# Two stacked layers with sign masks and low-rank adapters: the adapter's A beside W1's columns, layer 2 in three parts of 1040 columns

## The chip, the cores and the metric

The kernel runs on one core of a Trainium2 chip. The metric is the device time of one execution in microseconds (us); three executions of the kernel before gave 435.9, 437.23 and 437.77 us, median 437.23 us.

## The reference

`x` is [8, 256, 1024] in float32. For each of the eight batches b:

```
x = x + x @ W0.T + b0 + coeff[b] * (x @ (2*mask[b, :1024, :1024] - 1))          # layer 1
h = x @ A[id[b]].T                                                             # [256, 16]
x = x + x @ W1.T + b1 + h @ B[id[b]].T                                         # layer 2
```

`A` and `B` are the rank-16 adapters of the batch's id, W0 and W1 are 1024 x 1024. Everything is float32 in and out. The mask has a full 1024 x 1024 table of integers for each batch.

## The kernel before

Every float32 operand of a large product is split into a high part that the fp32r format holds and a rest (`whi`/`wlo`, `xhl`, `yhl`, `w1hi`/`w1lo`); a product is then three products: high by high, high by low, low by high. Layer 1 runs transposed: a step n = 8b + c makes 128 of batch b's 1024 features, for all 256 rows. `layer1(n)` (L620) issues, for each of eight k, one product of 512 columns (L631: `whi` against x's high and low halves side by side) and one of 256 (L633: `wlo` against the high half). Layer 2 of a step (m = n - 1, one step behind) is `adapter_h(m)` (L638, one product of 512 columns, L641: A's columns against y's halves) and four `layer2(m, st, oh)` (L646), where st is one of two row tiles and oh one of two halves of the 1024 output columns: three products of 512 columns each (L657, L658, L659), accumulated over the eight steps of a batch in banks 0 to 3 of PSUM. So a step has 16 + 1 + 12 products.

Where m is the last step of a batch, `finish` (L663) adds B's part and the bias by one product of 512 columns for each bank (L669): its stationary operand `ht` holds h in parts (rows 0 to 31, 32 to 63, 64 to 79 and 96 to 111) and rows of ones for the bias, its moving operand `bt` B's rows. It waits for `ht`, which ScalarE (`h_parts_hi`, L386, three instructions) and VectorE (`h_parts_lo`, L518) cut out of bank HB (6) when `adapter_h` is done.

Around these products a step n has these instructions on the other two engines, in this order (c = n mod 8):

- VectorE: `make_w(n+2)` (L499, coeff*sign + W0 over 1024 columns), at c = 5 and 7 `rows_lo` (L482) for the next batch's x, `chunk_lo(n+2)` (L505, the rest of W), `make_y(n)` (L511), `y_parts_lo(n)` (L515, which raises `y_lo`), and at c = 4 and 6 `turn_rows` (L476, transposes half of the next batch's x).
- ScalarE: at c = 5 and 7 `rows_hi` (L362), `chunk_hi(n+2)` (L351), `half_y(n)` (L377, after `layer1(n)` is done), `sign(n+3)` (L344, after the mask has landed), `y_parts_hi(n)` (L384). At c = 0 the h parts come before `y_parts_hi`, and two `move_z` (L401) and the sign come after it; VectorE has its own two `move_z` (L527) there. `move_z` copies a finished bank of 512 columns to SBUF.

All queues are written out by hand and are in order. SP issues a mask per step (L171; `load_mask(n+4)` waits for `chunk_lo(n)`), at c = 0 four stores of 512 columns (L216), then the six transfers of the next `bt` (L206, L207), and at c = 2 the next batch's x. The order that TensorE's queue has for a step is

```
layer1(n, ...)                      # 16 products
adapter_h(m)                        # waits y_lo of step m = n - 1
layer2(m, 0, 0); layer2(m, 0, 1); layer2(m, 1, 0)
if m % KT == KT - 1: finish(m // KT, 0, 0); finish(m // KT, 0, 1); finish(m // KT, 1, 0)
layer2(m, 1, 1)
```

Of the kernel before, what the change touches and what calls it, by code (L numbers as in the profile page):

```python
# [11 lines left out]
P = 128  # L12
# [4 lines left out]
def two_layer_kernel(nc, x, coeff, ids, mask, W0, b0, W1, b1, lora_a, lora_b, out):  # L17
# [38 lines left out]

    with ExitStack() as ctx:
# [7 lines left out]
        w1hi = sb("w1hi", [P, KT, D], F32R)  # L65
        w1lo = sb("w1lo", [P, KT, D], F32R)
# [16 lines left out]
        zst = sb("zst", [P, 4, HALF])  # L83
# [4 lines left out]
        at = sb("at", [P, KT, (NB + 3) * 2 * R], F32R)  # L88
# [25 lines left out]
        z_stored = [sem(f"z_stored{j}") for j in range(4)]  # L114
# [25 lines left out]
        l2_done = sem("l2_done")  # L140
        h_done = sem("h_done")
        h_hi = sem("h_hi")
# [7 lines left out]
        def part_views(u, part):  # L150

            kind, c, h, bank = units[u]
            src = ps[:, bank, :]
            if kind == "w1":
                return (w1hi, w1lo)[part][:, c, h * HALF:(h + 1) * HALF], src
            if kind == "a":
                dst = at[:, 4 * h:4 * h + 4, 0:2 * P].rearrange("p k (b two r) -> p k b two r", b=NB, two=2)
                return dst[:, :, :, part, :], src.rearrange("p (k b r) -> p k b r", k=4, b=NB)
            dst = bhl[:, part, :].rearrange("p (m o) -> p o m", o=KT)[:, 4 * h:4 * h + 4, :]
            return dst, src.rearrange("p (o m) -> p o m", o=4)  # L160

        @block.sync
        def _(sp):
# [35 lines left out]
            def load_bt(b):  # L199
                if b == 0:  # L200
                    sp.wait_ge(parts_lo, parted(number["b", 0, 1]))
                else:
                    sp.wait_ge(z_done, 4 * b)
# [5 lines left out]
            def store_z(b, st, oh):  # L209
                if oh == 0:  # L210
                    sp.wait_ge(z_moved_act, 2 * b + st + 1)
                else:
                    sp.wait_ge(z_moved_dve, 2 * b + st + 1)
                j = 2 * st + oh
                dst = out[b, st * P:(st + 1) * P, oh * HALF:(oh + 1) * HALF]
                sp.dma_start(dst, zst[:, j, :]).then_inc(z_stored[j], 16)  # L216
# [16 lines left out]
            for n in range(NS):  # L233
# [9 lines left out]
                if c == 0 and b > 0:  # L243
                    for st in range(ST):
                        for oh in range(2):
                            store_z(b - 1, st, oh)
                    load_bt(b)
                if c == 2 and b + 1 < NB:
                    load_x(b + 1)
            for st in range(ST):  # L250
                for oh in range(2):
                    store_z(NB - 1, st, oh)
            for j in range(4):
                sp.wait_ge(z_stored[j], 16 * NB)

        @block.gpsimd
        def _(pool):
# [30 lines left out]

            nc.gpsimd.memset(ident[:, :], 0.0).then_inc(ident_set, 1)
# [5 lines left out]
            nc.gpsimd.memset(at[:, :, 2 * P:].bitcast(F32), 0.0).then_inc(consts_set, 1)  # L295
# [26 lines left out]
            eye_w1(7)  # L322

        @block.scalar
        def _(act):
# [60 lines left out]
            def h_parts_hi(b):  # L386
                act.wait_ge(h_done, b + 1)
                if b == 0:
                    act.wait_ge(consts_set, 3)
                else:  # L390
                    act.wait_ge(z_done, 4 * b)
                nc.scalar.activation(ht[0:2 * R, :], ps[0:2 * R, HB, 0:S], ACT.Copy).then_inc(h_hi, 1)
                nc.scalar.activation(ht[64:64 + R, :], ps[0:R, HB, S:2 * S], ACT.Copy).then_inc(h_hi, 1)
                act.wait_ge(h_hi, 3 * b + 1)
                nc.scalar.activation(ht[96:96 + R, :], ht[0:R, :].bitcast(F32), ACT.Copy).then_inc(h_hi, 1)

            def move_z(b, st):
                act.wait_ge(z_done, 4 * b + 2 * st + 1)
                if b > 0:
                    act.wait_ge(z_stored[2 * st], 16 * b)  # L400
                nc.scalar.activation(zst[:, 2 * st, :], ps[:, Z0 + 2 * st, :], ACT.Copy).then_inc(z_moved_act, 1)  # L401
# [42 lines left out]
            for n in range(KT, NS):  # L444
# [6 lines left out]
                if c == 0:  # L451
# [3 lines left out]
                y_parts_hi(n)  # L455
                if c == 0:
# [4 lines left out]
            move_z(NB - 1, 0)  # L461
            move_z(NB - 1, 1)

        @block.vector
        def _(dve):
# [52 lines left out]
            def h_parts_lo(b):  # L518
                dve.wait_ge(h_hi, 3 * b + 2)
# [3 lines left out]
            def move_z(b, st):  # L523
                dve.wait_ge(z_done, 4 * b + 2 * st + 2)
                if b > 0:
                    dve.wait_ge(z_stored[2 * st + 1], 16 * b)
                nc.vector.tensor_copy(zst[:, 2 * st + 1, :], ps[:, Z0 + 2 * st + 1, :]).then_inc(z_moved_dve, 1)  # L527
# [36 lines left out]
            for n in range(KT, NS):  # L564
# [8 lines left out]
                if c == 0:  # L573
                    h_parts_lo(b - 1)
                y_parts_lo(n)
                if c == 0:
                    move_z(b - 1, 0)
                    move_z(b - 1, 1)
# [3 lines left out]
            move_z(NB - 1, 0)  # L582
            move_z(NB - 1, 1)

        @block.tensor
        def _(pe):
# [59 lines left out]
            def layer2(n, st, oh):  # L646
                b, c = divmod(n, KT)
                j = 2 * st + oh
                if c == 0 and b > 0:
                    if oh == 0:  # L650
                        pe.wait_ge(z_moved_act, 2 * (b - 1) + st + 1)
                    else:
                        pe.wait_ge(z_moved_dve, 2 * (b - 1) + st + 1)
                hi = yhl[:, n % 2, st * P:(st + 1) * P]
                lo = yhl[:, n % 2, S + st * P:S + (st + 1) * P]
                cols = slice(oh * HALF, (oh + 1) * HALF)
# [6 lines left out]
            def finish(b, st, oh):  # L663
                if st == 0 and oh == 0:
                    pe.wait_ge(h_hi, 3 * (b + 1))
                    pe.wait_ge(h_lo, b + 1)
                    pe.wait_ge(bt_in, 96 * (b + 1))
                    pe.wait_ge(bias_moved, 32)
                nc.tensor.matmul(ps[:, Z0 + 2 * st + oh, :], ht[:, st * P:(st + 1) * P],  # L669
                                 bt[:, oh * HALF:(oh + 1) * HALF], start=False, stop=True).then_inc(z_done, 1)  # L670

# [9 lines left out]
            for n in range(NS + 1):  # L681
# [26 lines left out]
                if m == 0:  # L708
                    pe.wait_ge(consts_set, 3)
# [46 lines left out]
```

## Time and profile before

| | |
|---|---|
| three runs, median | 437.23 us |
| the profiled execution's own time | 436.89 us |
| its span, first to last instruction | 435.2 us |
| mean granted TensorE clock | 0.991 |
| PE busy | 407.3 us (94%) |
| VectorE busy | 283.1 us (65%) |
| ScalarE busy | 237.4 us (55%) |

PE is TensorE's matmul, PEld its weight load, DVE is VectorE, ACT ScalarE, SPq SyncE's queue of DMA issues. A product's start is exact in the trace, its end is modelled and overlaps the next product's; so the cost of a product is read from one start to the next. Layer 1 of step n ends where the step's next product starts.

### The profile page before, as it was taken

What the parts mean: (1) busy time and instruction counts of PE and PEld (TensorE: products, weight loads), DVE (VectorE), ACT (ScalarE), POOL (GpSimd) and SP (SyncE); (2) the same over time, 40 slices, a digit from 0 to 9 for tenths busy, and PEclk for the clock granted to TensorE, in tenths of its full rate; (3) what the DMA queues carried; (4) which work ended last, traced back from release to release, by engine and by line L of the source; (5) the groups of instructions that cost most, each with busy time, mean ns of one, the idle gap of its engine ahead of it and who ended that gap; (6) DMA issues with size and microseconds to landing.
All of it is one profiled execution on the core that took longest, in us unless ns stands there. A gap on an engine that the chain in (4) does not pass through costs nothing.

```text
span 435.2 us, 5517 instructions
## 1 busy us (share of the span) xinstructions
PE 407.3 (94%) x2049; PEld 341.0 (78%) x2049; DVE 283.1 (65%) x334; ACT 237.4 (55%) x352; POOL 25.2 (6%) x47
## 2 busy tenths in 40 slices
PE   3649999788999999999999999999999999999996
PEld 3538878566888888888888888888888888888885
DVE  0455757786578756886578657876588658865512
ACT  3366666636555645665455754565565555665412
POOL 4334410000000000000000000000000000000000
PEclk9997999999999999999999999999999999999999
DMA  7995694615973299218942496319911793246002
GB/s 232 244 331 157 211 229 134 146 48 128 217 175 98 76 201 234 69 39 203 228 125 62 122 234 165 98 48 224 243 52 50 185 251 104 77 116 163 2 0 97
DMA packets 90846, 63.29 MB, mean 145 GB/s; under 512 B 3515, under 2 KB 84419, under 8 KB 90820
## 3 DMA queue, kind: packets, MB, share of 16 engines
q1 hardware_dynamic: 89588, 59.28, 55.5%
q0 software_dynamic: 1232, 3.67, 2.5%
q8 instruction: 16, 0.26, 0.2%
q14 instruction: 10, 0.08, 0.1%
HBM read 51.39 MB, written 8.39 MB: 137 GB/s over the span
## 4 chain that ended last, share of the span: by engine, by line
PE 82%; DMA 5%; DVE 5%; SPq 4%; ACT 2%; issue 1%; ACTq 0%; DVEq 0%
PE ps L631 25%; PE ps L633 13%; PE ps L658 13%; PE ps L657 12%; PE ps L659 12%; DMA wm<-in_mask_Bx4096x_ik_dram 5%; PE ps L641 3%; PE ps L617 2%; PE ps L669 2%; SPq L183 1%; DVE wm L499 1%; DVE w1lo L471 1%; SPq L190 1%; DVE wlo L505 1%; SPq L226 1%
## 5 line engine op out<-in xcount | busy, mean ns | idle before, releaser
L631 PE MATMUL ps<-xhl,whi 128*128 128x512 f32 x512 | 187.6, 405 | 1.9 <-DVE wlo L505 1.1
L633 PE MATMUL ps<-xhl,wlo 128*128 128x256 f32 x512 | 144.9, 283 | 0.0
L631 PEld LDWEIGHTS ps<-xhl,whi 128*128 128x128 f32 x512 | 97.8, 191 | 24.9 <-DVE wlo L505 1.3
L505 DVE TENSOR_TENSOR wlo<-wm,whi 128x1024 fp32r<-128x1024 f32 x64 | 79.2, 1238 | 48.6 <-ACT whi L351 48.6
L351 ACT ACTIVATE whi<-wm 128x1024 fp32r<-128x1024 f32 x64 | 67.8, 1059 | 75.0 <-DVE wm L499 73.7
L657 PE MATMUL ps<-w1hi,yhl 128*128 128x512 f32 x256 | 101.5, 396 | 0.0
L658 PE MATMUL ps<-w1lo,yhl 128*128 128x512 f32 x256 | 100.6, 393 | 0.0
L659 PE MATMUL ps<-w1hi,yhl 128*128 128x512 f32 x256 | 100.4, 392 | 0.0
L633 PEld LDWEIGHTS ps<-xhl,wlo 128*128 128x128 f32 x512 | 98.1, 192 | 2.4
L499 DVE SCALAR_TENSOR_TENSOR wm<-wm,cs,w0t 128x1024 f32<-128x1024 f32 x64 | 81.6, 1275 | 23.4 <-ACT w0t L329 12.4
L344 ACT ACTIVATE wm<-wm 128x1024 f32<-128x1024 int32 x64 | 67.4, 1054 | 9.6 <-DMA wm<-in_mask_Bx4096x_ik_dram 9.5
L659 PEld LDWEIGHTS ps<-w1hi,yhl 128*128 128x128 f32 x256 | 48.1, 188 | 10.6
L658 PEld LDWEIGHTS ps<-w1lo,yhl 128*128 128x128 f32 x256 | 48.1, 188 | 10.5
L657 PEld LDWEIGHTS ps<-w1hi,yhl 128*128 128x128 f32 x256 | 48.2, 188 | 7.8
L515 DVE TENSOR_TENSOR yhl<-ysum,yhl 128x256 fp32r<-128x256 f32 x64 | 27.3, 427 | 36.6 <-ACT yhl L384 36.5
L377 ACT ACTIVATE ysum<-ps,b0col 128x256 f32<-128x256 f32 x64 | 30.0, 468 | 33.6 <-PE ps L633 33.2
L511 DVE TENSOR_TENSOR ysum<-ps,ysum 128x256 f32<-128x256 f32 x64 | 26.9, 420 | 13.8 <-ACT ysum L377 13.7
L362 ACT ACTIVATE xhl<-xt 128x1024 fp32r<-128x1024 f32 x14 | 14.9, 1061 | 31.1 <-DVE xt L476 31.1
L384 ACT ACTIVATE yhl<-ysum 128x256 fp32r<-128x256 f32 x64 | 26.4, 413 | 8.4 <-DVE ysum L511 8.2
L476 DVE STREAM_TRANSPOSE xt<-xraw 128x1024 f32<-128x1024 f32 x14 | 30.6, 2183 | 0.0
L641 PE MATMUL ps<-yhl,at 128*128 128x512 f32 x64 | 25.4, 397 | 0.0
L617 PE MATMUL ps<-ident,w0raw 128*128 128x128 f32 x64 | 11.6, 320 | 10.8 <-POOL w0raw L262 5.4
(49 smaller groups left out, 186.9 us busy)
## 6 DMA issues: line engine op xcount, KB each, us to landing
wm<-in_mask_Bx4096x_ik_dram SPq DMA_DIRECT2D x64, 512.0 KB, 5.7
out_dram<-zst SPq DMA_DIRECT2D x32, 256.0 KB, 2.5
xraw<-in_x_dram SPq DMA_DIRECT2D x28, 256.0 KB, 7.3
w1raw<-_L_cond_base_weight_dram SPq DMA_DIRECT2D x8, 512.0 KB, 6.2
bt<-bhl SPq DMA_DIRECT2D x48, 64.0 KB, 2.9
w0raw<-in_L_cond_W_dram POOLq DMA_DIRECT2D x5, 512.0 KB, 6.9
w0raw<-in_L_cond_W_dram SPq DMA_DIRECT2D x3, 512.0 KB, 8.6
xrows<-in_x_dram SPq DMA_DIRECT2D x2, 512.0 KB, 6.6
```

The lines of the kernel that those rows point to most:

```text
L344: nc.scalar.activation(wm[:, s, :], wm[:, s, :].bitcast(I32), ACT.Copy, bias=-1.0, scale=2.0).then_inc(sign_made, 1)
L351: nc.scalar.activation(whi[:, n % WS, :, :], wm[:, n % MS, :].rearrange("p (k o) -> p k o", k=KT), ACT.Copy).then_inc(w_hi, 1)
L377: nc.scalar.activation(ysum[:, n % 2, :], ps[:, L1B + n % 2, S:2 * S], ACT.Identity, bias=b0col[:, n % KT:n % KT + 1]).then_inc(y_half, 1)
L476: nc.vector.transpose(xt[:, :, :].rearrange("p t (n q) -> p n t q", q=Q), xraw[:, :, :].rearrange("p n (i k) -> p n k i", k=KT)[:, :, g * ...
L499: nc.vector.scalar_tensor_tensor(chunk, chunk, cs[:, b:b + 1], w0t[:, c, :, :].rearrange("p k o -> p (k o)"), ALU.mult, ALU.add).then_inc( ...
L505: nc.vector.tensor_tensor(wlo[:, s, :, :], wm[:, n % MS, :].rearrange("p (k o) -> p k o", k=KT), whi[:, s, :, :].bitcast(F32), ALU.subtrac ...
L631: nc.tensor.matmul(ps[:, bank, :], whi[:, s, k, :], xhl[:, b % 2, k, :], start=(k == 0), stop=False, skip_group_check=True)
L633: op = nc.tensor.matmul(ps[:, bank, 0:S], wlo[:, s, k, :], xhl[:, b % 2, k, 0:S], start=False, stop=(k == KT - 1), skip_group_check=True)
L641: op = nc.tensor.matmul(ps[:, HB, :], at[:, c, b * 2 * R:b * 2 * R + P], yhl[:, n % 2, :], start=(c == 0), stop=(c == KT - 1))
L657: nc.tensor.matmul(ps[:, Z0 + j, :], hi, w1hi[:, c, cols], start=(c == 0), stop=False)
L658: nc.tensor.matmul(ps[:, Z0 + j, :], hi, w1lo[:, c, cols], start=False, stop=False)
L659: op = nc.tensor.matmul(ps[:, Z0 + j, :], lo, w1hi[:, c, cols], start=False, stop=False)
```

## The change

Batch 0 stays as it was. From batch 1 on, A's 16 columns stand beside W1's in `w1hi` and `w1lo` (ahead of them for even batches, behind them for odd ones), and the row of 1040 columns is cut at 352 and 696 into three parts (352, 344, 344), for two row tiles, so in six banks (0, 2, 3 and 1, 6, 7): 18 products a step instead of 1 + 12. Part j = 0 holds h's 16 columns. As h now has its rows on the partitions, ScalarE copies it to `h_row`, TensorE transposes it (two transposes into a free bank of layer 1), and ScalarE and VectorE make `ht` of that. The part j = 0 of a batch's last step is issued one step earlier: after layer 2 of the step before, and behind a wait for `y_lo` of this very step. `finish` is six products, `move_z` three per engine (328 to 352 columns each), and six stores. GpSimd copies A's columns to their place (`place_a`) once a batch.

```diff
+    WR = R + D + R
+    EDGES = (0, 352, 696, D + R)
+    ZB = ((0, 2, 3), (1, 6, 7))
...
-                if c == 0 and b > 0:
-                    for st in range(ST):
-                        for oh in range(2):
-                            store_z(b - 1, st, oh)
+                    for q in range(4 if b == 1 else 6):
+                        store_z(b - 1, q)
                     load_bt(b)
...
+            def place_a(b):
+                if b == 1:
+                    pool.wait_ge(parts_lo, parted(number["a", 0, 1]))
+                elif b >= 3:
+                    pool.wait_ge(l2_done, KT * (b - 1))
+                slot = 0 if b % 2 == 0 else R + D
+                for part, row in enumerate((w1hi, w1lo)):
+                    nc.gpsimd.tensor_copy(row[:, :, slot:slot + R],
+                                          at[:, :, (2 * b + part) * R:(2 * b + part + 1) * R].bitcast(F32)).then_inc(a_placed, 1)
...
+            def move_h(b):
+                act.wait_ge(h_done, b + 1)
+                if b >= 2:
+                    act.wait_ge(h_turned, b - 1)
+                cut = z_cut(b, 0)[3]
+                nc.scalar.activation(h_row[:, :, :], ps[:, ZB[0][0]:ZB[1][0] + 1, cut],
+                                     ACT.Copy).then_inc(h_moved, 1)
+
+            def h_parts_hi(b):
+                act.wait_ge(h_turned, b)
+                act.wait_ge(h_cleared, 1)
+                act.wait_ge(z_done, sums_before(b))
+                nc.scalar.activation(ht[0:R, :], ps[0:R, L1B + (KT * b + 9) % 2, 0:S], ACT.Copy).then_inc(h_hi, 1)
+                act.wait_ge(h_hi, h_hi_before(b) + 1)
+                nc.scalar.activation(ht[96:96 + R, :], ht[0:R, :].bitcast(F32), ACT.Copy).then_inc(h_hi, 1)
...
                 if c == 0:
-                    move_z(b - 1, 0)
-                    move_z(b - 1, 1)
                     sign(n + 3)
+                if c == 7:
+                    move_h(b)
...
+            def layer2(n, st, j):
...
+                cols = z_cut(b, j)[0]
+                dst = ps[:, ZB[st][j], 0:cols.stop - cols.start]
...
+                nc.tensor.matmul(dst, hi, w1hi[:, c, cols], start=(c == 0), stop=False, skip_group_check=True)
+                nc.tensor.matmul(dst, hi, w1lo[:, c, cols], start=False, stop=False, skip_group_check=True)
+                op = nc.tensor.matmul(dst, lo, w1hi[:, c, cols], start=False, stop=(c == KT - 1), skip_group_check=True)
...
+            def turn_h(b):
+                pe.wait_ge(h_moved, b)
+                for st in range(ST):
+                    op = nc.tensor.transpose(ps[0:R, L1B + (KT * b + 9) % 2, st * P:(st + 1) * P], h_row[:, st, :], ident[:, :])
+                op.then_inc(h_turned, 1)
...
+                pe.wait_ge(y_lo, m + 1)
+                if m % KT < KT - 1:
+                    for st in range(ST):
+                        for j in range(3):
+                            layer2(m, st, j)
+                else:
+                    if n < NS:
+                        turn_h(m // KT)
+                    layer2(m, 0, 1)
+                    layer2(m, 1, 1)
+                    if n == NS:
+                        turn_h(m // KT)
+                    layer2(m, 0, 2)
+                    layer2(m, 1, 2)
+                    for st in range(ST):
+                        for j in range(3):
+                            finish(m // KT, st, j)
+                if n < NS and n % KT == KT - 1:
+                    pe.wait_ge(y_lo, n + 1)
+                    layer2(n, 0, 0)
+                    layer2(n, 1, 0)
```

How TensorE's queue changes, at two places, and SP's at one. First TensorE where batch 1's step 15 (c = 7) has had its layer 1 and layer 2 of step 14 ends. Before, the next thing is layer 1 of step 16:

```order
L658 MATMUL ps<-w1lo,yhl 128x512
L659 MATMUL ps<-w1hi,yhl 128x512
L657 MATMUL ps<-w1hi,yhl 128x512
L658 MATMUL ps<-w1lo,yhl 128x512
L659 MATMUL ps<-w1hi,yhl 128x512
L631 MATMUL ps<-xhl,whi 128x512 [waits x_lo,y_made,w_lo]
L633 MATMUL ps<-xhl,wlo 128x256
```

After, six products of step 15 itself come between, behind a wait for `y_lo` (L765 to L767 are the three products of `layer2`, L723 and L725 those of `layer1`):

```order
L765 MATMUL ps<-w1hi,yhl 128x352
L766 MATMUL ps<-w1lo,yhl 128x352
L767 MATMUL ps<-w1hi,yhl 128x352
L765 MATMUL ps<-w1hi,yhl 128x344 [waits y_lo]
L766 MATMUL ps<-w1lo,yhl 128x344
L767 MATMUL ps<-w1hi,yhl 128x344
L765 MATMUL ps<-w1hi,yhl 128x344
L766 MATMUL ps<-w1lo,yhl 128x344
L767 MATMUL ps<-w1hi,yhl 128x344
L723 MATMUL ps<-xhl,whi 128x512 [waits x_lo,y_made,w_lo]
L725 MATMUL ps<-xhl,wlo 128x256
```

The wait for step 15's `y_lo`, which stood behind layer 1 of step 16, now stands ahead of it. Second, TensorE at the end of a batch, from the last products of layer 2 to the first of the next step. Before:

```order
L657 MATMUL ps<-w1hi,yhl 128x512
L658 MATMUL ps<-w1lo,yhl 128x512
L659 MATMUL ps<-w1hi,yhl 128x512
L669 MATMUL ps<-bt,ht 128x512 [waits bt_in,bias_moved,h_lo,h_hi]
L669 MATMUL ps<-bt,ht 128x512 x2
L657 MATMUL ps<-w1hi,yhl 128x512
L658 MATMUL ps<-w1lo,yhl 128x512
L659 MATMUL ps<-w1hi,yhl 128x512
L669 MATMUL ps<-bt,ht 128x512
L631 MATMUL ps<-xhl,whi 128x512 [waits y_made,w_lo]
```

After, with the two transposes of h (L776) twelve products of layer 2 earlier:

```order
L725 MATMUL ps<-xhl,wlo 128x256
L776 MATMUL ps<-ident,h_row 16x128 [waits h_moved,y_lo]
L776 MATMUL ps<-ident,h_row 16x128
L765 MATMUL ps<-w1hi,yhl 128x344
L766 MATMUL ps<-w1lo,yhl 128x344
L767 MATMUL ps<-w1hi,yhl 128x344
```

The transposes stand right behind layer 1 of the next step. And TensorE's queue where those twelve products end:

```order
L765 MATMUL ps<-w1hi,yhl 128x352
L766 MATMUL ps<-w1lo,yhl 128x352
L767 MATMUL ps<-w1hi,yhl 128x352
L794 MATMUL ps<-bt,ht 128x328 [waits bt_in,h_lo,h_hi]
L794 MATMUL ps<-bt,ht 128x344
L794 MATMUL ps<-bt,ht 128x352
L794 MATMUL ps<-bt,ht 128x328
L794 MATMUL ps<-bt,ht 128x344
L794 MATMUL ps<-bt,ht 128x352
L723 MATMUL ps<-xhl,whi 128x512 [waits y_made,w_lo]
```

`finish` is six products in a row, with nothing of layer 2 between them. Third, SP's queue at the very end of the kernel. Before:

```order
L171 DMA wm<-in_mask_Bx4096x_ik_dram 128x8x128 [waits w_lo] x3
L216 DMA out_dram<-zst 128x512 [waits z_moved_act]
L216 DMA out_dram<-zst 128x512 [waits z_moved_dve]
L216 DMA out_dram<-zst 128x512 [waits z_moved_act]
L216 DMA out_dram<-zst 128x512 [waits z_moved_dve]
L57 UNCONDITIONAL_BRANCH [waits z_stored2,z_stored3,z_stored1,z_stored0]
```

After:

```order
L208 DMA wm<-in_mask_Bx4096x_ik_dram 128x8x128 [waits w_lo] x3
L253 DMA out_dram<-zst 128x328 [waits z_moved_act]
L253 DMA out_dram<-zst 128x344 [waits z_moved_dve]
L253 DMA out_dram<-zst 128x352 [waits z_moved_act]
L253 DMA out_dram<-zst 128x328 [waits z_moved_dve]
L253 DMA out_dram<-zst 128x344 [waits z_moved_act]
L253 DMA out_dram<-zst 128x352 [waits z_moved_dve]
L89 UNCONDITIONAL_BRANCH [waits z_stored1,z_stored0]
```

Four stores became six.

## Rows read from the trace of the kernel before

**Rows 1.** The page: busy time, and the slices of the span.
```profile
PE 407.3 (94%) x2049; PEld 341.0 (78%) x2049; DVE 283.1 (65%) x334; ACT 237.4 (55%) x352; POOL 25.2 (6%) x47
...
PE   3649999788999999999999999999999999999996
...
POOL 4334410000000000000000000000000000000000
PEclk9997999999999999999999999999999999999999
```

**Rows 2.** Timeline, TensorE, steps 9 to 16 and 28 to 32 (start us, us, engine line).
```profile
105.31 0.40 PE L641 MATMUL ps<-yhl,at 128*128 128x512 f32 x1
...
145.90 0.40 PE L641 MATMUL ps<-yhl,at 128*128 128x512 f32 x1
...
217.55 0.40 PE L641 MATMUL ps<-yhl,at 128*128 128x512 f32 x1
...
229.16 0.40 PE L641 MATMUL ps<-yhl,at 128*128 128x512 f32 x1
...
234.98 0.39 PE L641 MATMUL ps<-yhl,at 128*128 128x512 f32 x1
...
237.95 0.39 PE L631 MATMUL ps<-xhl,whi 128*128 128x512 f32 x1
...
240.76 0.40 PE L641 MATMUL ps<-yhl,at 128*128 128x512 f32 x1
```

**Rows 3.** Timeline, VectorE, steps 28 to 31 (last brackets: idle before, releaser).
```profile
219.51 0.43 DVE L515 TENSOR_TENSOR yhl<-ysum,yhl 128x256 fp32r<-128x256 f32 x1 [0.83 <-ACT yhl L384]
219.85 2.18 DVE L476 STREAM_TRANSPOSE xt<-xraw 128x1024 f32<-128x1024 f32 x1
...
231.16 0.43 DVE L515 TENSOR_TENSOR yhl<-ysum,yhl 128x256 fp32r<-128x256 f32 x1 [0.48 <-ACT yhl L384]
231.51 2.19 DVE L476 STREAM_TRANSPOSE xt<-xraw 128x1024 f32<-128x1024 f32 x1
...
238.04 0.43 DVE L515 TENSOR_TENSOR yhl<-ysum,yhl 128x256 fp32r<-128x256 f32 x1 [0.48 <-ACT yhl L384]
```

**Rows 4.** Timeline, the last batch's last step: TensorE and VectorE.
```profile
424.33 0.39 PE L641 MATMUL ps<-yhl,at 128*128 128x512 f32 x1
...
425.94 0.42 DVE L515 TENSOR_TENSOR yhl<-ysum,yhl 128x256 fp32r<-128x256 f32 x1 [0.48 <-ACT yhl L384]
```

**Rows 5.** Timeline, batch 0's finish: what TensorE waited for.
```profile
100.33 0.41 DVE L520 TENSOR_TENSOR ht<-ps,ht 32x256 fp32r<-32x256 f32 x1
...
100.84 0.94 PE L669 MATMUL ps<-bt,ht 128*128 128x512 f32 x3 [1.57 <-ACT ht L395]
```

**Rows 6.** Timeline, ScalarE and VectorE at a batch's first step (c = 0).
```profile
240.96 0.47 ACT L377 ACTIVATE ysum<-ps,b0col 128x256 f32<-128x256 f32 x1 [0.21 <-PE ps L633]
...
242.11 0.42 ACT L395 ACTIVATE ht<-ht 16x256 fp32r<-16x256 f32 x1
242.38 0.41 DVE L520 TENSOR_TENSOR ht<-ps,ht 32x256 fp32r<-32x256 f32 x1
```

**Rows 7.** Timeline, TensorE: four transposes of 128 columns and what follows.
```profile
81.98 0.66 PE L617 MATMUL ps<-ident,w1raw 128*128 128x128 f32 x4 [0.80 <-DVE bhl L471]
82.39 0.48 PE L657 MATMUL ps<-w1hi,yhl 128*128 128x512 f32 x1
```

**Rows 8.** Timeline, the end of the kernel: TensorE, ScalarE, VectorE, SP.
```profile
429.57 0.84 PE L669 MATMUL ps<-bt,ht 128*128 128x512 f32 x3
430.00 1.09 ACT L401 ACTIVATE zst<-ps 128x512 f32<-128x512 f32 x2 [1.06 <-PE ps L669]
...
430.93 0.39 PE L669 MATMUL ps<-bt,ht 128*128 128x512 f32 x1
431.36 0.69 DVE L527 COPY zst<-ps 128x512 f32<-128x512 f32 x1 [0.44 <-PE ps L669]
```

**Rows 9.** SP's queue: the store issues, and the last one's start.
```profile
L216 SPq DMA_DIRECT2D out_dram<-zst x32: 337/430/952, 102.0 to 432.1; - x32
...
432.07 0.35 SPq L216 DMA_DIRECT2D out_dram<-zst  x1
```

**Rows 10.** ScalarE's longest wait for a mask in a steady batch.
```profile
160.87 1.06 ACT L344 ACTIVATE wm<-wm 128x1024 f32<-128x1024 int32 x1 [1.75 <-DMA wm<-in_mask_Bx4096x_ik_dram]
```

More of the change, by code:

```diff
@@ L55, in x_split, with z_cut, sums_before, moves_before @@
         return 4 + 2 * (b - 1) + g + 1
+    def z_cut(b, j):
+        g = j if b % 2 == 0 else 2 - j
+        lo, hi = EDGES[g], EDGES[g + 1]
+        if b % 2 == 0:
+            skip = R if j == 0 else 0
+            return slice(lo, hi), slice(skip, hi - lo), slice(lo + skip - R, hi - R), slice(0, R)
+        end = hi - R if j == 0 else hi
+        return slice(R + lo, R + hi), slice(0, end - lo), slice(lo, end), slice(hi - lo - R, hi - lo)
+    def sums_before(b):
+        return 4 + 6 * (b - 1) if b else 0
+    def moves_before(b):
+        return 2 + 3 * (b - 1) if b else 0
+    def stores_before(b):
+        return 2 + 3 * (b - 1) if b else 0
+    def h_hi_before(b):
+        return 3 + 2 * (b - 1) if b else 0
     with ExitStack() as ctx:
@@ L113, in two_layer_kernel @@
         bt_in = sem("bt_in")
-        z_stored = [sem(f"z_stored{j}") for j in range(4)]
+        z_stored = [sem(f"z_stored{st}") for st in range(ST)]
         ident_set = sem("ident_set")
@@ L249, in _ @@
                     load_x(b + 1)
+            for q in range(6):
+                store_z(NB - 1, q)
             for st in range(ST):
[L251 to L254, printed above, removed]
+                sp.wait_ge(z_stored[st], 16 * stores_before(NB))
         @block.gpsimd
@@ L322, in _ @@
             eye_w1(7)
+            place_a(1)
+            place_a(2)
+            pool.wait_ge(z_done, sums_before(1))
+            nc.gpsimd.memset(ht[0:80, :].bitcast(F32), 0.0).then_inc(h_cleared, 1)
+            for b in range(3, NB):
+                place_a(b)
         @block.scalar
@@ L450, in _ @@
                 half_y(n)
-                if c == 0:
+                if c == 0 and b == 1:
+                    first_h_parts_hi()
+                elif c == 0:
                     h_parts_hi(b - 1)
@@ L572, in _ @@
                 make_y(n)
-                if c == 0:
+                if c == 0 and b == 1:
+                    first_h_parts_lo()
+                elif c == 0:
                     h_parts_lo(b - 1)
                 y_parts_lo(n)
-                if c == 0:
-                    move_z(b - 1, 0)
-                    move_z(b - 1, 1)
+                if c == 0 and b == 1:
+                    first_move_z(0)
+                    first_move_z(1)
+                elif c == 0:
+                    for q in (1, 3, 5):
+                        move_z(b - 1, q)
                 if c in (4, 6) and b + 1 < NB:
@@ L581, in _ @@
             h_parts_lo(NB - 1)
-            move_z(NB - 1, 0)
-            move_z(NB - 1, 1)
+            for q in (1, 3, 5):
+                move_z(NB - 1, q)
         @block.tensor
@@ L670, in finish @@
                                  bt[:, oh * HALF:(oh + 1) * HALF], start=False, stop=True).then_inc(z_done, 1)
+            def finish(b, st, j):
+                if st == 0 and j == 0:
+                    pe.wait_ge(h_hi, h_hi_before(b + 1))
+                    pe.wait_ge(h_lo, b + 1)
+                    pe.wait_ge(bt_in, 96 * (b + 1))
+                _, cut, cols, _ = z_cut(b, j)
+                nc.tensor.matmul(ps[:, ZB[st][j], cut], ht[:, st * P:(st + 1) * P], bt[:, cols],
+                                 start=False, stop=True, skip_group_check=True).then_inc(z_done, 1)
             pe.wait_ge(ident_set, 2)
```

163 lines of the change are left out of this document (98 added, 65 removed).

## The prediction, made before the changed kernel was run

> **What bounds the kernel now.** I read the page first: TensorE is busy for 94% of the span; from the tenth slice (98 us) on every slice is at 9 tenths or more and the granted clock at 9 tenths or more, while VectorE is at 65% and ScalarE at 55% [rows 1]. So the time is what TensorE issues, plus whatever it is made to wait for. A change that shortens its list pays in full, and a change that makes it wait costs in full, unless something else was going to be late. Then I read the timeline, for the price of a product. A step is 5.80 us (seven steps between the first two rows, 40.59 us), of which layer 1's sixteen products take 2.81 us and the thirteen products of 512 columns (adapter and layer 2) the other 2.99 us on average [rows 2]. Third, I read how late y comes: `y_lo` of step n is raised by VectorE's L515. At c = 4 that instruction starts 1.96 us after the end of layer 1 (217.55 to 219.51); at c = 7 it starts 3.06 us after it (234.98 to 238.04) [rows 2, 3]. Today this costs nothing, since TensorE asks for it only after layer 2 of the step before (2.99 us) and layer 1 of the next (2.81 us): 5.8 us of cover.
>
> **What the shorter list gives.** 56 steps (batches 1 to 7) go from thirteen products with 6656 columns to eighteen with 6240: 416 columns less, five products more. What a product costs beside its columns decides, and two groups of the trace give two equations: 16 products and 6144 columns are 2.81 us, 13 products and 6656 columns are 2.99 us [rows 2]. They solve to 0.425 ns a column and 12.5 ns a product. Then a layer 2 is 18 x 0.0125 + 6240 x 0.000425 = 2.88 us, 0.11 us less a step, **-6.4 us** in all. The two ends: if the cost is by columns alone at layer 2's own rate, 2.99 x 6240/6656 = 2.80 us, -0.19 us a step, -10.5 us. If the columns run at the full 2.4 GHz and all the rest (2.99 - 2.77 = 0.22 us over thirteen) is by product, 17 ns each, 18 products are 2.90 us, -0.09 us a step, -5.0 us. I take the fit of both equations; layer 1, with more products per column, is dearer per column than layer 2 (0.457 against 0.449 ns), which speaks against columns alone.
>
> The Trainium skill states another split ("TensorE: Matmul & The Clock Gate", section "Wait — 56ns, not 53.3ns?"): once warm, a product starts N columns / 2.4 GHz + about 2.5 ns after the one before. By that a product of 512 columns would be 216 ns, where this case's rows have 230 ns on average, so the trace does not agree on the size; with the page's 2.5 ns the five more products would cost almost nothing and the term would be -9.0 us.
>
> **The new wait, at every c = 7.** The part with h's columns of a batch's last step now stands behind layer 2 of the step before and ahead of the next layer 1, behind a wait for this step's `y_lo`. Of 5.8 us of cover 2.88 us are left. When does `y_lo` come? The rounds of VectorE and ScalarE from c = 4 to c = 7 are a chain of their own: two of them hold a transpose of x of 2.2 us, and L515 goes from 219.51 to 238.04, 18.53 us for three rounds where TensorE takes 17.43 us [rows 2, 3]. That chain does not get shorter when TensorE's steps do, so at c = 7 it is later by 3 x 0.11 us: L515 starts 3.06 + 0.34 = 3.40 us after layer 1. From the start of such a VectorE instruction to the TensorE product that waited for it is 0.51 us (100.33 to 100.84) [rows 5]. So the wait ends at 3.91 us and the cover at 2.88 us: TensorE stands for 1.03 us. That holds in batches 1 to 6. In batch 7 no next x is transposed, L515 starts 1.61 us after layer 1 [rows 4], and 1.61 + 0.51 us lie inside the cover. Six times 1.03 us: **+6.2 us**. Its ends go with the columns' term: with -0.19 us a step the drift is 0.56 us and the cover 2.80 us, 1.33 us each, +8.0 us; with -0.09 us it is 0.94 us each, +5.6 us. Behind the waiting products stands layer 1 of the next batch; nobody else hurries, since VectorE and ScalarE catch up meanwhile. I expect no fall of the clock: after TensorE's wait of 1.57 us at 100.84 us [rows 5] the granted clock stayed in its highest tenth [rows 1].
>
> **Transposes of h.** Two of 128 columns per batch, seven batches. Four such transposes take 0.41 us [rows 7], so two are 0.2 us: **+1.4 us** (0.7 if the few stationary columns make them cheaper, 2.1 if the change of kind costs). Their wait for `h_row` has all of a layer 1 (2.81 us) as cover against ScalarE's one copy: nothing.
>
> **Finish.** Four products of 512 columns become six with the same 2048 columns: two products' fixed part, 7 x 0.025 us, **+0.2 us** (0 to 0.3). Its wait for `ht`: half_y starts 0.20 us after layer 1 and today the h parts follow until VectorE's L520 at 242.38, 1.62 us after 240.76 [rows 2, 6]; the new chain is one ScalarE instruction shorter, so ready by about 1.6 us, and the cover is 0.2 + 12 x 0.16 = 2.1 us. Nothing, but if `half_y` were late by over 0.5 us the wait would show. In the last batch the transposes stand only six products (0.95 us) ahead of `finish`, and a copy, the rest and the hand-over take about 1.1 us: +0.2 us.
>
> **The end.** Three copies per engine instead of two, then six stores. The first copy starts 0.43 us after the first finish product [rows 8]; with some 0.5 us for it SP begins 0.9 us after that product, and a store's issue takes 0.43 us [rows 9], so the sixth begins at 0.9 + 5 x 0.43 = 3.1 us, which is 2.3 us after the last product started. Today that is 432.07 - 430.93 = 1.14 us [rows 8, 9]. **+1.2 us** (0.5 if smaller stores issue faster, 1.5). The six copies of a steady batch lie beside layer 1 of the next step, which today has the four.
>
> **What I price at nothing.** GpSimd's copies of A (a whole batch early, and its engine is idle from the seventh slice on [rows 1]). SP's two more stores make the next mask's issue some 0.4 us later; ScalarE already waits up to 1.75 us for a mask at c = 2 [rows 10]. A longer wait there makes y late for two or three steps, and what is left of it at c = 7 adds to the new wait. VectorE's rounds without a transpose give back about 1 us a step, so mostly nothing is left: 0, at worst +2 us.
>
> **Sum.** -6.4 + 6.2 + 1.4 + 0.2 + 0.2 + 1.2 = +2.8 us against the profiled execution's own 436.89 us: 439.7 us. That execution is 0.34 us below the median of the three runs, so against the median the forecast is +2.5 us, 0.6% slower. A difference under 0.5% (2.2 us) cannot be told from none here, and the forecast stands just beyond it.
>
> **The rivals.**
>
> *Columns pay in full, the wait eats them.* Terms at the other end: -10.5 + 8.0 + 1.4 + 0 + 0.2 + 1.2 = +0.3 us, 437.2 us, no difference. For it: layer 2's rate alone; against it: layer 1's dearer columns. By the rule of the Trainium skill's page above a step would be 0.16 us shorter, the wait 1.2 us, and the sum, as an estimate, +1.3 us.
>
> *y is in time at c = 7.* The place is the wait behind layer 2 of step c = 6, and it decides at 2.88 us after layer 1: if the chain of L505, L511, L384, L515 ends before, there is no wait, and -6.4 + 3.0 = -3.4 us give 433.5 us, faster; with the columns' full price 429.2 us. It would need a chain 1 us shorter than rows 3 have; what could shorten it is that the batch's c = 0 and c = 4 rounds run ahead of TensorE further than I let them. Against it: `make_y` and `half_y` can't start before layer 1 is done, and at c = 4 the chain is as early as it can be (1.96 us).
>
> *The lateness is carried on.* Masks later by the two stores, ScalarE held at c = 7 by its wait for `h_done`, three copies at c = 0: the chain would start c = 4 already late, and the wait at c = 7 grows to 1.5 us or more: +3 us more, 442.7 us. For it: ScalarE's wait for a mask at c = 2, up to 1.75 us already [rows 10]. Against it: between c = 2 and c = 4 there are two rounds without a transpose, in which VectorE gains on TensorE.
>
> *The change does not do what it says*, adapter products still issued: excluded by the queue's order, which holds none from batch 1's steps on.
>
> **How the numbers follow.** Forecast case (439.7 us, half a microsecond beyond what can be told apart) 0.46, of which a third falls within 0.5% and the rest is slower; columns in full 0.24, no difference; y in time 0.14, faster; lateness carried on 0.16, slower. That makes 0.14 faster, 0.39 within 0.5%, 0.47 slower. The predicted time is the forecast's. The range leaves out most of the faster rival and the far end of the slower one: 435.4 to 442.4 us.
>
> **What would show it.** In the profile after: TensorE's idle ahead of L765 put down to VectorE's y parts, about 1 us six times and none in batch 7; a steady layer 2 of 2.88 us (2.80 or 2.90 would show the other ends) and steps of 5.69 us; transposes L776 0.1 us each; about 2.3 us between the last L794 and the last store's issue. I am wrong if the wait ahead of L765 is missing or far from 1 us, or if a step is shorter by other than about 0.1 us.

## The result, and the profile after

The changed kernel takes 450.35 us (median of four runs, 448.82 to 453.57), the kernel before 437.5 us (median of four). The ratio is 1.031, with a 95% interval of 1.027 to 1.034: slower by 3%, and outside the range of 435.4 to 442.4 us. The sign was forecast, the size was not: +2.5 us became +13 us.

The profiled execution took 449.86 us, its span is 448.2 us where before it was 435.2 us. The lines of the page that answer to [rows 1]:

```profile
PE 407.2 (91%) x2357; PEld 370.2 (83%) x2357; DVE 281.7 (63%) x341; ACT 236.0 (53%) x359; POOL 29.1 (6%) x61
...
PE   3659998979999999979998999899998999799995
...
PEclk9688999999999999989999999999998999989998
```

The busy time of TensorE did not fall (a busy product that is modelled to overlap the next is no measure of its cost), but where the row of tenths was all nines from 109 us on, up to the last slice, it now has five notches, one for each wait at c = 7 listed below except the first (142.57 us), and in the granted clock three notches stand in steady batches that were not there.

Is a step shorter? TensorE's timeline, two neighbouring steps of the changed kernel (start us, us, engine line): layer 1 begins, layer 2 begins, the next layer 1 begins.

```profile
101.90 0.40 PE L723 MATMUL ps<-xhl,whi 128*128 128x512 f32 x1
...
104.67 0.32 PE L765 MATMUL ps<-w1hi,yhl 128*128 128x344 f32 x1
...
107.53 0.39 PE L723 MATMUL ps<-xhl,whi 128*128 128x512 f32 x1
```

It is: layer 2 takes 2.86 us here and 2.85 us in most steps, where thirteen products took 2.99 us [rows 2], and layer 1 takes 2.78 us in 31 of 55 steps and 2.81 to 2.83 us in most others, instead of 2.81. A step is 5.63 to 5.66 us instead of 5.80.

So the loss is in waits. The longest of them, by engine waited for (engine, line, waited for: total, times, longest):

```profile
ACT wm L395 <- DMA wm<-in_mask_Bx4096x_ik_dram: 21.9, 14, 4.0
...
PE ps L765 <- DVE yhl L592: 12.8, 7, 2.9
```

The second row is the wait the prediction named, at double its size. The first is what made it so (run 2 below shows it): before, ScalarE's waits for masks were

```profile
ACT wm L344 <- DMA wm<-in_mask_Bx4096x_ik_dram: 9.5, 10, 2.5
```

The seven PE waits of the second row, in TensorE's timeline, are these (in the last bracket the idle time before). Six are at c = 7; the one at 164.53 us is the ordinary layer 2 of batch 2's c = 2:

```profile
142.57 0.43 PE L765 MATMUL ps<-w1hi,yhl 128*128 128x344 f32 x1 [1.10 <-DVE yhl L592]
...
164.53 0.43 PE L765 MATMUL ps<-w1hi,yhl 128*128 128x352 f32 x1 [0.75 <-DVE yhl L592]
...
193.08 0.61 PE L765 MATMUL ps<-w1hi,yhl 128*128 128x352 f32 x1 [2.90 <-DVE yhl L592]
...
242.93 0.42 PE L765 MATMUL ps<-w1hi,yhl 128*128 128x344 f32 x1 [1.73 <-DVE yhl L592]
...
291.24 0.43 PE L765 MATMUL ps<-w1hi,yhl 128*128 128x352 f32 x1 [1.68 <-DVE yhl L592]
...
339.98 0.65 PE L765 MATMUL ps<-w1hi,yhl 128*128 128x344 f32 x1 [2.18 <-DVE yhl L592]
...
390.56 0.43 PE L765 MATMUL ps<-w1hi,yhl 128*128 128x352 f32 x1 [2.48 <-DVE yhl L592]
```

In batch 7 there is none, as forecast. Two of them are followed by products of 0.61 and 0.65 us instead of 0.43: the clock had fallen. The stretches around the longest wait and around the 1.73 us one, with the granted clock in the third column from the end (stretch, length, busy time of PE, PEld, DVE, ACT and POOL, clock, DMA share, GB/s):

```profile
187.16:193.00 5.84, 3.02 (x20) 2.73 (x18) 5.36 (x7) 3.85 (x5) 0.00 (x0) 1.00 0.20 61
193.00:194.95 1.95, 1.87 (x6) 1.88 (x7) 1.22 (x2) 0.00 (x0) 0.00 (x0) 0.54 0.00 0
194.95:198.52 3.57, 3.57 (x17) 3.04 (x17) 1.23 (x1) 1.14 (x2) 0.00 (x0) 0.77 0.02 5
238.19:243.99 5.80, 4.07 (x27) 3.78 (x26) 5.32 (x6) 3.80 (x5) 0.00 (x0) 1.00 0.00 1
243.99:246.81 2.82, 2.82 (x17) 2.42 (x17) 1.30 (x2) 1.15 (x2) 0.00 (x0) 1.00 0.01 3
```

Behind the wait of 2.90 us the six products run at 0.54 of full speed (near 1.2 GHz, the lower level) and take 1.87 us up to the start of the next layer 1, and that layer 1 takes 3.57 instead of 2.8 us. Behind the wait of 1.73 us the clock stays full: the six products take 1.06 us (242.93 to 243.99; 0.95 us where nothing is waited for), the layer 1 behind them 2.82 us. The waits of 2.18 and 2.48 us have a layer 1 of 3.47 and 3.97 us behind them.

**Where y comes late.** The rows that answer to [rows 3], in batch 3: layer 1 ends at 221.30 (c = 4) and at 238.19 (c = 7).

```profile
221.30 0.32 PE L765 MATMUL ps<-w1hi,yhl 128*128 128x344 f32 x1
...
223.88 0.42 DVE L592 TENSOR_TENSOR yhl<-ysum,yhl 128x256 fp32r<-128x256 f32 x1 [1.04 <-ACT yhl L435]
...
238.19 0.32 PE L765 MATMUL ps<-w1hi,yhl 128*128 128x344 f32 x1
...
242.44 0.43 DVE L592 TENSOR_TENSOR yhl<-ysum,yhl 128x256 fp32r<-128x256 f32 x1 [0.48 <-ACT yhl L435]
```

y starts 2.58 us after layer 1 at c = 4 (1.96 before) and 4.25 us at c = 7 (3.06 before). The same reading of all six batches gives, at c = 2 / 4 / 7: 2.96 / 1.96 / 3.63, 6.05 / 3.76 / 5.44, 3.70 / 2.58 / 4.25, 3.73 / 2.56 / 4.21, 4.71 / 3.03 / 4.71, 5.06 / 3.33 / 5.01 us. What is over 1.96 us at c = 4 is over 3.63 us at c = 7, within 0.02 us: VectorE's chain hands a lateness through both transposes. And the lateness starts at c = 2, at a mask, the longest wait of which answers to [rows 10]:

```profile
162.65 1.06 ACT L395 ACTIVATE wm<-wm 128x1024 f32<-128x1024 int32 x1 [3.98 <-DMA wm<-in_mask_Bx4096x_ik_dram]
```

**Why the mask is late.** SP's queue behind a batch's end, first before (in batch 4's first step, whose layer 1 ended at 240.76), then after (in batch 4's, whose layer 1 ended at 246.81, and in batch 5's, whose layer 1 ended at 295.12; start us, us, queue and line, transfer, count):

```profile
244.14 1.84 SPq L216 DMA_DIRECT2D out_dram<-zst  x4
246.03 3.12 SPq L206 DMA_DIRECT2D bt<-bhl  x5
249.19 0.59 SPq L207 DMA_DIRECT2D bt<-bhl  x1
249.83 1.33 SPq L171 DMA_DIRECT2D wm<-in_mask_Bx4096x_ik_dram  x2
```

After, batch 4:

```profile
249.75 2.83 SPq L253 DMA_DIRECT2D out_dram<-zst  x6
252.62 3.12 SPq L243 DMA_DIRECT2D bt<-bhl  x5
255.79 0.59 SPq L244 DMA_DIRECT2D bt<-bhl  x1
256.42 1.36 SPq L208 DMA_DIRECT2D wm<-in_mask_Bx4096x_ik_dram  x2
```

Batch 5:

```profile
298.06 2.81 SPq L253 DMA_DIRECT2D out_dram<-zst  x6
300.92 3.91 SPq L243 DMA_DIRECT2D bt<-bhl  x5
304.87 0.59 SPq L244 DMA_DIRECT2D bt<-bhl  x1
305.51 1.37 SPq L208 DMA_DIRECT2D wm<-in_mask_Bx4096x_ik_dram  x2
```

In batch 4 the masks are issued 9.6 us after that layer 1 instead of 9.1 us, in batch 5 10.4 us after it. Over batches 2 to 7 the issue is 1.7, 0.4, 0.5, 1.4, 1.9 and 0.1 us later than in the same batch before. The large ones have one single issue that is long: a store of 1.12 us in batch 2 (the batch of the 3.98 us wait, where the six stores' issues took 3.63 us) and of 1.86 us in batch 6, a transfer of B's rows of 1.37 us in batch 5; a usual store's issue takes 0.34 to 0.48 us.

At the same time ScalarE asks for the mask earlier: six of the last step's products now stand ahead of that layer 1, so c = 0 is shorter by 0.9 us, and two more steps by 0.15 us each. In batch 2 ScalarE was ready for it 13.2 us after that layer 1 ([rows 10]: 160.87 less the wait of 1.75 us, against 145.90) and is now at 12.2 us (162.65 less 3.98, against 146.46); the other five batches have 1.0 to 1.2 us earlier as well. So the earlier asking is there in every batch, and in three of six it is the larger half.

### The profile page after: what moved, and what is told of

It is laid out like the page before. It is cut to its first block, busy times and chain, and to the rows that moved or that the text cites. A ratio compares the mean times of both kernels' runs of the same rounds, so it can differ in the third digit from the quotient of the medians.

```text
span 448.2 us, 6201 instructions
## 1 busy us (share of the span) xinstructions
PE 407.2 (91%) x2357; PEld 370.2 (83%) x2357; DVE 281.7 (63%) x341; ACT 236.0 (53%) x359; POOL 29.1 (6%) x61
## 4 chain that ended last, share of the span: by engine, by line
PE 35%; DVE 29%; DMA 13%; SPq 11%; ACT 7%; issue 4%; DVEq 0%; ACTq 0%
DMA wm<-in_mask_Bx4096x_ik_dram 13%; PE ps L723 10%; DVE wlo L582 7%; DVE xt L553 6%; DVE wm L576 6%; PE ps L725 5%; PE ps L765 5%; PE ps L767 4%; PE ps L766 4%; DVE xhl L559 4%; SPq L243 3%; ACT yhl L435 2%; ACT whi L402 2%; PE ps L709 2%; SPq L253 2%
## 5 line engine op out<-in xcount | busy, mean ns | idle before, releaser
L723 PE MATMUL ps<-xhl,whi 128*128 128x512 f32 x512 | 189.4, 407 | 1.7 <-DVE wlo L582 0.9
L725 PE MATMUL ps<-xhl,wlo 128*128 128x256 f32 x512 | 145.5, 284 | 0.0
L765 PE MATMUL ps<-w1hi,yhl 128*128 128x344 f32 (+1 forms) x336 | 109.9, 327 | 12.8 <-DVE yhl L592 12.8
L723 PEld LDWEIGHTS ps<-xhl,whi 128*128 128x128 f32 x512 | 99.2, 194 | 22.5 <-DVE wlo L582 1.2
L767 PE MATMUL ps<-w1hi,yhl 128*128 128x344 f32 (+1 forms) x336 | 108.7, 323 | 0.0
L766 PE MATMUL ps<-w1lo,yhl 128*128 128x344 f32 (+1 forms) x336 | 108.6, 323 | 0.0
L725 PEld LDWEIGHTS ps<-xhl,wlo 128*128 128x128 f32 x512 | 99.5, 194 | 0.4
L765 PEld LDWEIGHTS ps<-w1hi,yhl 128*128 128x128 f32 x336 | 63.7, 190 | 17.2 <-DVE yhl L592 14.9
L766 PEld LDWEIGHTS ps<-w1lo,yhl 128*128 128x128 f32 x336 | 64.0, 190 | 0.0
L767 PEld LDWEIGHTS ps<-w1hi,yhl 128*128 128x128 f32 x336 | 63.9, 190 | 0.0
L709 PEld LDWEIGHTS ps<-ident,w0raw 128*128 128x128 f32 x64 | 10.1, 202 | 11.0 <-issue 5.5
```

The costliest lines, as they stand in the source:

```text
L709: op = nc.tensor.transpose(ps[:, bank, m * P:(m + 1) * P], cut[m], ident[:, :])
L723: nc.tensor.matmul(ps[:, bank, :], whi[:, s, k, :], xhl[:, b % 2, k, :], start=(k == 0), stop=False, skip_group_check=True)
L725: op = nc.tensor.matmul(ps[:, bank, 0:S], wlo[:, s, k, :], xhl[:, b % 2, k, 0:S], start=False, stop=(k == KT - 1), skip_group_check=True)
L765: nc.tensor.matmul(dst, hi, w1hi[:, c, cols], start=(c == 0), stop=False, skip_group_check=True)
L766: nc.tensor.matmul(dst, hi, w1lo[:, c, cols], start=False, stop=False, skip_group_check=True)
L767: op = nc.tensor.matmul(dst, lo, w1hi[:, c, cols], start=False, stop=(c == KT - 1), skip_group_check=True)
```

## The experiments

### 1 and 3. h's part in its usual place; and the mask ahead of the stores too

```diff
                 else:
-                    if n < NS:
-                        turn_h(m // KT)
+                    layer2(m, 0, 0)
+                    layer2(m, 1, 0)
                     layer2(m, 0, 1)
                     layer2(m, 1, 1)
-                    if n == NS:
-                        turn_h(m // KT)
+                    turn_h(m // KT)
...
-                if n < NS and n % KT == KT - 1:
-                    pe.wait_ge(y_lo, n + 1)
-                    layer2(n, 0, 0)
-                    layer2(n, 1, 0)
```

with `move_h` in ScalarE's queue moved to c = 0, ahead of the h parts. The second edit is

```diff
-                if n + 4 < NS:
+                if n + 4 < NS and not (c == 1 and b > 0):
                     load_mask(n + 4)
+                if c == 0 and b > 0:
+                    load_mask(n + 5)
```

Expected of the first edit alone:

> The changed kernel, but the part with h's columns of a batch's last step is issued in its usual place, after layer 1 of the next step, so no wait for y ahead of layer 1; the transposes of h come twelve products into it. Wait theory (the waits for y at c = 7, 15.7 us more than the products in the changed kernel's trace, and the fallen clock behind three of them, are the loss): both go, steps stay at 5.64 us, the wait of finish for h is at most 0.3 us a batch; 430 to 434 us, faster than before. Rival (the shorter steps themselves outrun VectorE, ScalarE or the masks, and the wait only shows where it bites first): waits turn up ahead of layer 1 or of layer 2, 440 us or more.

Expected of both:

> Both edits at once. Wait theory: as with the first edit alone, 430 to 434 us, within 1 us of it, since late masks cost nothing where nobody waits for y. Rival: a further gain of several us, if late masks also cost elsewhere.

Measured: 438.17 us for the first alone (ratio to before 1.001, 0.998 to 1.004), 431.82 us for both (0.988, 0.984 to 0.992). The wait ahead of layer 1 is gone in both, but 438 us fits neither theory's number (in kind it is the rival: waits turn up elsewhere), and the two runs differ by 6 us where the wait theory had said 1. The first edit's waits:

```profile
ACT wm L395 <- DMA wm<-in_mask_Bx4096x_ik_dram: 24.5, 12, 4.0
...
PEld ps L765 <- DVE yhl L592: 3.3, 6, 1.1
PEld ps L776 <- ACT h_row L450: 3.2, 4, 0.9
PEld ps L794 <- ACT ht L459: 3.2, 7, 0.6
```

and those of both:

```profile
PEld ps L796 <- ACT ht L461: 1.8, 7, 0.3
...
ACT wm L397 <- DMA wm<-in_mask_Bx4096x_ik_dram: 2.5, 2, 1.5
```

So late masks cost without the early wait as well. In the first edit's trace TensorE's layer 2 waits for y at c = 2 (y 5.3 to 6.1 us after layer 1 in four batches, where 5.6 us is all the cover of a step), and at c = 0 y comes 4.3 to 4.5 instead of 3.6 us after layer 1 in four batches, which makes the transposes wait for `h_row` and `finish` for `ht`. With the masks early, y comes 3.63 us after layer 1 at c = 7 and 1.96 us at c = 3 and 4, in every batch. That version is faster than the kernel before.

### 2. The mask ahead of the stores, h's part as in the change

The second edit above, alone. Expected:

> The changed kernel, with one move in SP's queue: at c = 0 the mask of step n + 5 is issued ahead of the stores and B's rows instead of behind them. Theory that the masks' issue is what made y late: ScalarE's waits for a mask at c = 2 nearly vanish, L592 at c = 7 starts some 3.5 us after layer 1 instead of 3.6 to 5.4, the wait is about 1.2 us six times as the prediction had it, the clock stays; about 439 us. Rival (masks are late because the DMA engines are full, or y is late by ScalarE's own hold at c = 7): 448 us or more.

Measured: 440.69 us (ratio 1.006, 1.004 to 1.008), 10 us less than the changed kernel. The two waits:

```profile
PE ps L767 <- DVE yhl L594: 6.6, 6, 1.1
...
ACT wm L397 <- DMA wm<-in_mask_Bx4096x_ik_dram: 5.4, 3, 2.4
```

All six waits are alike now: from the end of layer 1 to the next layer 1 it is 5.17 to 5.19 us, where 24 products take 3.80 us, so 1.37 us each, with y at 3.62 to 3.65 us. No layer 1 takes longer than 2.83 us: no fallen clock. This is the wait as the prediction had priced it, 8.2 us in place of 6.2. ScalarE's hold at c = 7 (its wait for `h_done`) is still there and was not what made y late: run 3, where it is gone, has y at 3.63 to 3.65 us at c = 7 too. By the two traces, from step 9 to the last product of `finish`, this run is 10.9 us shorter than the changed kernel, and what the account below puts down to late masks (5.5 us of longer waits, 0.9 us at c = 2, 4.6 us of fallen clock) is 11.0 us.

Against the kernel before this run is at +3.0 us, near the +2.8 us of the prediction's sum. That is luck in part: the gain of the shorter list and the cost of the wait were both priced some 2 us too small, and the two errors cancel.

### 4. The kernel before, with the wait alone

```diff
                 if m % KT == KT - 1:
                     finish(m // KT, 1, 1)
+                if n > KT and n < NS and n % KT == KT - 1:
+                    pe.wait_ge(y_lo, n + 1)
```

> The kernel before with nothing but the wait: at c = 7 of batches 1 to 7 TensorE waits for this step's y between layer 2 of the step before and layer 1 of the next. By the rows of before (L515 3.06 us after layer 1, 0.51 us to TensorE, cover 2.99 us) 0.6 us six times, +3.5 us, 441 us. If the lateness feeds on itself through the masks, more: 443 us or above.

Measured: 440.42 us (ratio 1.005, 1.002 to 1.009), +2.7 us. Its waits:

```profile
PEld ps L631 <- DVE yhl L515: 5.0, 6, 1.0
...
PE ps L631 <- DVE yhl L515: 2.5, 6, 0.6
```

The layer 2 stretch at c = 7 is 3.50 to 3.56 us in five batches and 3.72 in one, against 2.99, and layer 1 behind it 2.93 instead of 2.81: 0.7 us a batch, 3.8 us in all by the trace, 2.7 us by the medians (five executions from 440.22 to 441.42 us, of which the traced one is 441.25). The wait is a cost by itself, without anything of the new columns; without the shorter steps and the six stores it stays small.

### 5. One store for each row tile

```diff
+            def store_rows(b, st):
+                sp.wait_ge(z_moved_act, moves_before(b) + 2 + st)
+                sp.wait_ge(z_moved_dve, moves_before(b) + 1 + 2 * st)
+                sp.dma_start(out[b, st * P:(st + 1) * P, :], zst[:, st, :]).then_inc(z_stored[st], 16)
...
-                    for q in range(4 if b == 1 else 6):
-                        store_z(b - 1, q)
+                    if b == 1:
+                        for q in range(4):
+                            store_z(0, q)
+                    else:
+                        for st in range(ST):
+                            store_rows(b - 1, st)
                     load_bt(b)
...
```

> The changed kernel, with one store for each row tile of 128 x 1024 (batches 1 to 7) in place of three: SP's stores at c = 0 should take under 1.5 us instead of 2.8 to 4.7, so the next masks are issued 1.5 to 3 us sooner. If the two extra stores are what made the masks late, ScalarE's waits for masks fall from 22 to under 10 us, the wait for y at c = 7 to 1.4 us six times, no fallen clock: 439 to 441 us. If it is B's rows (3.7 us of issues) and the shorter c = 0 step, most of it stays: 445 us or more.

Measured: 440.61 us (ratio 1.005, 1.003 to 1.008). The wait rows, and SP's queue in one batch:

```profile
ACT wm L404 <- DMA wm<-in_mask_Bx4096x_ik_dram: 16.6, 13, 2.6
...
PE ps L774 <- DVE yhl L601: 8.4, 6, 1.6
```

```profile
201.44 1.12 SPq L258 DMA_DIRECT2D out_dram<-zst  x2
202.61 3.74 SPq L243 DMA_DIRECT2D bt<-bhl  x5
206.40 0.59 SPq L244 DMA_DIRECT2D bt<-bhl  x1
207.03 1.34 SPq L208 DMA_DIRECT2D wm<-in_mask_Bx4096x_ik_dram  x2
```

The stores' issues are 1.1 us, and the time is what the first alternative said. But the masks' waits fell to 16.6, not under 10 us. The masks are issued 8.8 to 9.8 us after the layer 1 of c = 0, in four of six batches sooner than before (9.0 to 9.5 us). What is left in every batch is that ScalarE asks 1.0 us earlier; B's rows take 4.2 to 5.2 us here (3.7 before), and in two batches the mask can be used only 5.0 and 5.3 us after its issue instead of 4.1 to 4.5. It is enough to keep the waits at 1.37 to 1.88 us, and none of them has a slow layer 1 behind it. By the two traces 9.2 us lie between this run and the changed kernel, from step 9 to the last product of `finish`: 4.6 us of fallen clock, 3.7 us of shorter waits at c = 7 and 0.9 us of the wait at c = 2.

### 6 and 7. The best version; and h's part in the middle of layer 1

Run 6 is run 3 with the stores of run 5. Run 7 is run 6 with h's part put elsewhere:

```diff
...
-                    layer1(n, range(3, 6))
+                    if n % KT == 0 and n > KT:
+                        layer1(n, range(3, 4))
+                        pe.wait_ge(y_lo, n)
+                        layer2(n - 1, 0, 0)
+                        layer2(n - 1, 1, 0)
+                        layer1(n, range(4, 6))
+                    else:
+                        layer1(n, range(3, 6))
...
```

> The fastest version so far (h's part in its usual place, mask issued ahead of the stores) with one store for each row tile. The masks are in time already, so only the end can gain: one issue behind the last copy instead of a queue of six: 1 us less, 430.5 to 431.5 us. No change would mean that the end is bound by the last copy and its landing.

> As the run beside it, but h's part of a batch's last step is issued in the middle of the next step's layer 1 (after four of its eight pairs), behind its wait for y. Cover is then 2.85 + 1.4 = 4.25 us against y's L592 at 3.63 + 0.59 us after layer 1. Wait theory: no wait for y, and the small waits of finish for h (about 0.1 us a batch) go: 0 to 1 us less than the run beside it. If it is slower by 3 us or more, it is not the wait's place but the splitting off of h's part that costs.

Measured: 431.98 us (0.986, 0.984 to 0.988) and 431.38 us (0.985, 0.981 to 0.988). Run 6 is no faster than run 3 by its median. By the traces its end, counted from the start of the last product, is 4.8 us instead of 5.5 us, a gain smaller than the spread of the runs (3 to 5 us each). Run 7 bears out that it is the place of the wait that costs: the same six products ahead of the same transposes, 1.4 us later, and no row has TensorE waiting for y. Runs 6 and 7 can't be told apart by their medians.

### 8. The kernel before, with the mask ahead of the stores

> The kernel before with the mask of step n + 5 issued ahead of the stores at c = 0. Its TensorE never waits for y or for late weights after batch 0, so this should be worth nothing: 437 to 438 us. A gain would mean that the mask's place helps by itself, in all versions.

Measured: 437.49 us (0.999, 0.997 to 1.002). Early masks are worth nothing where nobody waits for y; in the versions above they are worth 6 us and 10 us.

## Why the prediction was wrong

From the start of step 9 to the last product of `finish` the changed kernel takes 340.7 us, the kernel before 328.4 us, 12.3 us more. By stretches: layers 2 -7.9, layers 1 -0.7, waits at c = 7 +8.2 with y at the 3.63 us that it has with masks in time and +5.5 for what masks made later, the wait for y at batch 2's c = 2 +0.9, fallen clock +4.6 (2.03 in h's products, 2.53 in the layers 1 behind), transposes +1.5, the last wait for h +0.2, finish +0.3; the rest, -0.3, is not assigned. The end adds 1.4 us (5.6 instead of 4.2 us from the start of the last product), batch 0 came out 0.6 us shorter; together the 13.0 us of the two spans. All this is one trace of each kernel. The mean granted clock of the changed kernel's four executions is 0.971 (the traced one), 0.979, 0.967 and 0.982, so how much the clock falls differs from one to the next.

- **The shorter list**: priced at -6.4 us, measured -7.9 (2.85 for 2.88 us a step), -8.6 with layer 1. With 13 products and 6656 columns at 2.99 us and 18 and 6240 at 2.85 us the two equations give 0.434 ns a column and 8 ns a product, not 0.425 and 12.5. The Trainium skill ("TensorE: Matmul & The Clock Gate", section "Wait — 56ns, not 53.3ns?") has N / 2.4 GHz + about 2.5 ns a product; by that, as an estimate, these 18 products would take 2.65 us. They take 2.85 us, so this trace does not agree either.
- **The wait at c = 7** was priced 6 x 1.03 us. With masks in time it is 6 x 1.37 us (run 2): y at 3.63 instead of 3.40 us, mostly since the steps shrank by 0.17 and not 0.11 us, and then 0.48 us from VectorE to TensorE (142.09 to 142.57; 0.51 priced), but the first product behind the idle time takes 0.27 us to the next start instead of 0.16 us. That last 0.11 us was not in the sum. Run 4 shows the same: layer 1 behind the wait is 0.12 us longer. The mechanism, its place and its absence in batch 7 were right.
- **The step that failed** is the one that priced SP's two stores, and with them the whole way from a mask to y, at nothing: "the next mask's issue some 0.4 us later" and "mostly nothing is left". For the issue alone 0.4 us was right in three of six batches (0.1 to 0.5 us); in the other three it is 1.4 to 1.9 us, with a single issue of 1.1 to 1.9 us in each. What I had overlooked is that the same edit shortens c = 0, so that ScalarE asks 1.0 us earlier in every batch. The price of a wait is the sum of both: ScalarE waits 1.6 to 4.0 us at c = 2, before 0.1 to 1.8 us. And the "about 1 us a step" that VectorE gives back was 0.85 us (a round of 4.79 us in steps of 5.64), and a second wait for a mask at c = 4 (0.3 to 0.7 us) took of it in four batches: from 3.7 us and more at c = 2, two rounds did not reach 1.96 us. This was the rival "the lateness is carried on", priced at +3 us with a chance of 0.16. It cost 5.5 us directly, 0.9 us at c = 2 and, through the clock, 4.6 us. Of the rival's three reasons the masks were the one: ScalarE's hold did nothing (run 2), and what the three copies add at c = 1 (y at 3.18 instead of 2.55 us) is down to 2.3 us at c = 2 and gone at c = 3 when the masks are in time.
- **The clock.** "I expect no fall of the clock" held for the new waits up to 1.7 us (the row before had 1.57 us) and not for those of 2.2 to 2.9 us. It is a second cost that only the grown wait brings: runs 2 and 5, where TensorE stands idle for 1.6 us at most, have none.
- **Transposes** 7 x 0.14 us up to the next product, which then takes 0.24 instead of 0.16 us: 1.5 us (1.4 priced). **Finish** 0.93 us against 0.91, and 0.2 us in the last batch. **The last batch's wait** for h 0.2 us (0.2 priced). **The end** +1.4 us (1.2 priced).
- **The rivals**: columns in full (-10.5 us) and y in time did not happen. No adapter product is left from batch 1 on.
- **A misreading** on which nothing hung: TensorE's tenth slice before stands at 8 tenths; nines go from the eleventh (109 us) to the last but one.

What stays open: why a single issue in SP's queue, now a store, now a transfer of B's rows, takes 1.1 to 1.9 us in some batches (2.1 us in run 5), so that six stores take 2.8 us in one batch and 3.6 to 4.7 us in another; no run isolates it.

## What to carry to other kernels

When products are moved ahead of a wait, read how late the awaited value comes at exactly that step, add what each shorter step takes from the cover, and then ask of every in-order queue what it issues late: a transfer's issue that slips by 1 us and a user that comes 1 us earlier make 2 us. A wait of which the base part is known can grow until the clock falls behind it as well; so first put the transfer that feeds the chain ahead of the ones nobody waits for. The gain of a shorter list was real here, 1.2 to 1.5% below the kernel before, once nothing waited inside the cover.

## What the runs showed of the hardware

TensorE's granted clock fell to the lower level after idle times of 2.2, 2.5 and 2.9 us in the middle of dense work and stayed full after those of 1.1 to 1.7 us; I had expected it full throughout. These are three falls in one execution. In between lies an idle time of 1.9 us in batch 0, which all ten traces have at 77 to 82 us: in run 4 the clock fell 1.3 us behind it (0.50 of full speed from 80.3 to 83.7 us), in the other nine it stayed full, so at that length the idle time alone does not decide. Run 4's row of tenths, with the fall in the eighth slice:

```profile
PEclk9788999899999999999999999999999999999999
```

A fall cost 0.4 to 0.8 us in the six products behind the wait and 0.6 to 1.1 us in the layer 1 after them. At full clock the first product behind a wait of 1.1 us took 0.27 us to the next start, where such products otherwise take 0.16 us. And layer 1, whose products the change does not touch, took 2.78 us in 31 of 55 steps instead of 2.81; no run says why.
